# Attention in one kernel: four PSUM banks for scores, three single banks for transposed scores, exponentials one head at a time

## The reference

```python
N_HEADS = 32; N_KV = 8; HEAD_DIM = 8; N_GROUPS = 4      # 4 query heads share a key-value head
q = einsum('bsd,ed->bse', x, Wq) ...; k, v likewise; q, k = _apply_rope(q, k, s)
scores = jnp.einsum('bkgqd,bkld->bkgql', qg, k) * SCALE
attn = jax.nn.softmax(scores, axis=-1)
out = jnp.einsum('bkgql,bkld->bkgqd', attn, v)
x = x + einsum('bsd,ed->bse', out, Wo)                  # x was normalised before q, k, v
```

## Time and profile before

| what | value |
|---|---|
| time, median of three runs | 1677.78 us (1677.04 to 1677.88) |
| the profiled execution | 1684.23 us, its span 1682.4 us |
| TensorE matmuls / weight loads busy | 1460.8 / 1021.4 us of the span |
| VectorE / ScalarE / GpSimd busy | 1089.4 / 846.8 / 489.9 us |
| reductions of score chunks (L918), largest group | 305.4 us, 684 ns each |
| exponentials (L1059) | 247.9 us, 1022 ns each |

### The profile page before, as it was taken

How to read it: one execution, slowest core, us unless ns; L and a number is a source line. 1 busy time by engine, 2 the same in 40 slices (tenths; PEclk the granted TensorE clock), 3 DMA queues, 4 the chain that set the end, 5 groups by cost and what they waited for, 6 DMA issues and landing times. The chain is left out here.

```text
span 1682.4 us, 24339 instructions
## 1 busy us (share of the span) xinstructions
PE 1460.8 (87%) x7712; PEld 1021.4 (61%) x7712; DVE 1089.4 (65%) x1946; ACT 846.8 (50%) x1206; POOL 489.9 (29%) x409
## 2 busy tenths in 40 slices
PE   3999369999999966999497987899999999998697
PEld 3566243333333334665386775788888887887586
DVE  4122379999999953112476775777787778777375
ACT  1222115777777741221432776666756675765332
POOL 1344310000000021443100113556556556565100
PEclk9999778999999996999799998899999999999799
DMA  8432201111111009222301002323222323231200
GB/s 298 132 49 45 56 20 23 27 27 27 27 27 27 8 22 340 45 45 40 103 1 33 26 22 82 94 76 101 80 87 85 94 77 104 68 103 38 76 1 26
DMA packets 83008, 111.79 MB, mean 66 GB/s; under 512 B 11905, under 2 KB 60801, under 8 KB 82913
## 3 DMA queue, kind: packets, MB, share of 16 engines
q1 hardware_dynamic: 73536, 96.44, 19.4%
q0 software_dynamic: 9376, 14.16, 4.8%
HBM read 89.99 MB, written 11.93 MB: 61 GB/s over the span
## 5 line engine op out<-in xcount | busy, mean ns | idle before, releaser
L918 DVE TENSOR_REDUCE attn_max_chunks<-attn_scores 128x1 f32<-128x512 f32 x488 | 305.4, 684 | 23.9 <-PE attn_scores L1147 23.8
L1059 ACT ACTIVATE attn_probs<-attn_scoresT 128x1024 f32<-128x1024 f32 x256 | 247.9, 1022 | 122.3 <-PE attn_scoresT L1163 122.1
L1147 PE MATMUL attn_scores<-attn_k_picks,attn_q_group 64*128 64x512 f32 x488 | 185.8, 462 | 10.9 <-DVE attn_max_chunks L918 2.3
L1147 PEld LDWEIGHTS attn_scores<-attn_k_picks,attn_q_group 64*128 64x128 f32 x488 | 85.0, 190 | 173.2 <-DVE attn_max_chunks L918 164.8
L1577 DVE SCALAR_TENSOR_TENSOR ssm_scan_x<-ssm_scan_proj,ssm_w_conv,ssm_scan_x 128x1023 f32<-128x1023 f32 (+2 forms) x96 | 123.0, 1282 | 79.5 <-ACT ssm_scan_x L1572 73.8
L1163 PE MATMUL attn_scoresT<-attn_q_group,attn_k_picks 64*128 64x512 f32 x512 | 151.7, 433 | 3.3 <-ACT attn_probs L1059 3.3
L401 DVE TENSOR_TENSOR moe_h<-moe_silu,moe_up 128x512 f32<-128x512 f32 x46 | 31.7, 688 | 188.4 <-PE moe_up L516 188.4
L1175 PE MATMUL attn_o<-attn_probs,attn_v_group 128*32 128x512 f32 x1024 | 138.0, 611 | 0.4 <-ACT attn_probs L1059 0.3
L62 PE MATMUL ssm_scan_proj<-ssm_xnT_hi,ssm_w_in_hi 128*128 128x512 f32 x256 | 109.6, 428 | 23.2 <-DVE ssm_scan_x L1577 21.4
L448 ACT ACTIVATE moe_silu<-moe_gate 128x512 f32<-128x512 f32 x46 | 27.5, 597 | 199.6 <-PE moe_gate L516 199.6
L286 POOL DMA_INDIRECT moe_sums<-moe_y,moe_token x46 | 72.7, 1581 | 164.8 <-DVE moe_y L410 158.9
(11 more groups left out here) (338 smaller groups left out, 3193.1 us busy)
## 6 DMA issues: line engine op xcount, KB each, us to landing
ssm_cum_all<-ssm_cums SPq DMA_DIRECT2D x32, 512.0 KB, 3.8
ssm_scan_exp_cum<-ssm_cums SPq DMA_DIRECT2D x32, 512.0 KB, 3.7
moe_w_gate_up<-in_moe_w SPq DMA_DIRECT2D x16, 512.0 KB, 11.3
moe_w_up<-in_moe_w SPq DMA_DIRECT2D x16, 512.0 KB, 11.2
moe_w_down<-in_moe_w SPq DMA_DIRECT2D x16, 512.0 KB, 11.5
ssm_w_in<-in_in_w SPq DMA_DIRECT2D x64, 128.0 KB, 2.7
ssm_scan_w_out<-in_out_w SPq DMA_DIRECT2D x8, 512.0 KB, 3.8
moe_sums<-main_residual SPq DMA_DIRECT2D x2, 1024.0 KB, 5.6
```

The lines of the kernel that those rows point to most:

```text
L918: return nc.vector.tensor_reduce(rmaxc[:, half, place:place + 1], chunk_bank(g, n), AX_X, ALU.max).then_inc(reduced, 1)
L1059: nc.scalar.activation(probs[s % 2][:, 2 * pair:2 * pair + 2, :], st_ps[pair][:], ACT.Exp, scale=SCALE).then_inc(exp_done, 1)
L1147: nc.tensor.matmul(chunk_bank(g, n), qs[b][head_rows(j), t * P:(t + 1) * P], kz[b][head_rows(j), j % 2, c * BANK:(c + 1) * BANK], start=Tr ...
```

## The change

The pair banks for transposed scores become three single banks, and the bank that this frees is the fourth for chunks. Each transposed-scores matmul now signals for itself, and each exponential reads one head (128x512), four to a slot. The heads of the transposed scores and of the values matmuls are ordered by `T_TURNS`. A slot's order on TensorE becomes: head 0, chunk, head 1, chunk, head 2, chunk, values of the slot before, head 3, chunk. The banks of the lead-in are given out anew, and in the last group ScalarE reads the first final transposes (`last_high(0)`) one slot later.

```diff
+T_TURNS = (2, 0, 3, 1)
-        st_ps = [sp.ps(f"scoresT{b}", [P, 2, BANK]) for b in range(2)]
+        st_ps = [sp.ps(f"scoresT{b}", [P, BANK]) for b in range(3)]
+        fourth_ps = sp.ps("scores3", [P, BANK])
-        ring = [mx_ps[0], mx_ps[1], third_ps]
+        ring = [mx_ps[0], mx_ps[1], third_ps, fourth_ps]
-        bank_of, free_from = {}, [0, 1, 2]
+        bank_of, free_from = {}, [0, 1, 2, 3]
-            free_from[bank] = k + 3
+            free_from[bank] = k + len(ring)
+        st_bank, st_before = [], []
+        for k in range(GQ * SLOTS):
+            st_bank.append(1 if k == GQ * SLOTS - 1 else k % 3)
+        for k in range(GQ * SLOTS):
+            back = 1
+            while st_bank[k - back] != st_bank[k]:
+                back += 1
+            st_before.append(back)
-            return n % 2 if n >= LEAD_SCORES_T else (3, 5, 0, 1, 4, 6)[n % 6]
+            return (0, 1, 3)[n % 3] if n >= LEAD_SCORES_T else (4, 5, 0, 1, 6, 3)[n % 6]
...
-                    sync.wait_ge(scoresT_done, 2 * SLOTS * (g - 1))
+                    sync.wait_ge(scoresT_done, GQ * SLOTS * (g - 1))
...
-            def exp_pair(g, s, pair):
+            def exp_head(g, s, i):
                 n = SLOTS * g + s
-                act.wait_ge(scoresT_done, 2 * n + pair + 1)
-                if not (isinstance(n, int) and n < 2):
+                act.wait_ge(scoresT_done, GQ * n + i + 1)
+                if i == 0 and not (isinstance(n, int) and n < 2):
                     act.wait_ge(pv_done, n - 1)
-                nc.scalar.activation(probs[s % 2][:, 2 * pair:2 * pair + 2, :], st_ps[pair][:], ACT.Exp,
+                nc.scalar.activation(probs[s % 2][:, i, :], st_ps[st_bank[GQ * s + i]][:], ACT.Exp,
                                      scale=SCALE).then_inc(exp_done, 1)
...
-                    if last and s == KT_TILES + 1:
+                    if last and s == KT_TILES + 2:
                         last_high(0)
...
-            def scoresT(g, b, s, pair, after=None):
+            def scoresT(g, b, s, i):
...
-                    pe.wait_ge(exp_done, 2 * n - 1 + pair)
+                    pe.wait_ge(exp_done, GQ * n + i + 1 - st_before[k])
+                j = T_TURNS[i]
+                nc.tensor.matmul(st_ps[st_bank[k]][:], kz[b][head_rows(j), j % 2, kt * P:(kt + 1) * P],
+                                 qs[b][head_rows(j), half_cols(half)], start=True, stop=True).then_inc(scoresT_done, 1)
...
-                pe.wait_ge(exp_done, 2 * (SLOTS * g + s) + 2)
+                pe.wait_ge(exp_done, GQ * (SLOTS * g + s) + GQ)
...
-                    scoresT(g, b, s, 0)
-                    scoresT(g, b, s, 1, jobs(2))
-                    jobs(1)
-                    if s > 0:
-                        values(g, b, s - 1)
-                    elif not first:
-                        values(g - 1, 1 - b, SLOTS - 1)
+                    for i in range(GQ):
+                        if i == GQ - 1:
+                            if s > 0:
+                                values(g, b, s - 1)
+                            elif not first:
+                                values(g - 1, 1 - b, SLOTS - 1)
+                        scoresT(g, b, s, i)
+                        jobs(1)
                     jobs(len(todo))
```

More of the change, by code:

```diff
@@ L1149, in score_chunk @@
                                  start=True, stop=True).then_inc(scores_done, 1)
-            def scoresT(g, b, s, pair, after=None):
+            def scoresT(g, b, s, i):
                 half, kt = divmod(s, KT_TILES)
-                n = SLOTS * g + s
-                if pair == 0 and kt == 0:
+                n, k = SLOTS * g + s, GQ * s + i
+                if i == 0 and kt == 0:
                     pe.wait_ge(max_in[half], 32 * (g + 1))
-                if isinstance(n, int) and n == 0:
+                if isinstance(n, int) and n == 0 and i < 3:
                     pe.wait_ge(reduced, LEAD_SCORES_T)
                 else:
-                    pe.wait_ge(exp_done, 2 * n - 1 + pair)
-                upper = after is not None and TURNS[after % GQ] < 2
-                for i in ((1, 0) if upper else (0, 1)):
-                    j = TURNS[2 * pair + i]
-                    last = nc.tensor.matmul(st_ps[pair][:, i, :], kz[b][head_rows(j), j % 2, kt * P:(kt + 1) * P],
-                                            qs[b][head_rows(j), half_cols(half)], start=True, stop=True)
-                last.then_inc(scoresT_done, 1)
+                    pe.wait_ge(exp_done, GQ * n + i + 1 - st_before[k])
+                j = T_TURNS[i]
+                nc.tensor.matmul(st_ps[st_bank[k]][:], kz[b][head_rows(j), j % 2, kt * P:(kt + 1) * P],
+                                 qs[b][head_rows(j), half_cols(half)], start=True, stop=True).then_inc(scoresT_done, 1)
             def values(g, b, s):
                 half, kt = divmod(s, KT_TILES)
-                pe.wait_ge(exp_done, 2 * (SLOTS * g + s) + 2)
+                pe.wait_ge(exp_done, GQ * (SLOTS * g + s) + GQ)
                 if s == 0:
@@ L1222, in jobs @@
                     def jobs(count):
-                        after = None
                         for kind, ahead, n in todo[:count]:
@@ L1266, in _ @@
                 score_chunk(0, 0, n)
-            for bank in range(3, 7):
+            for bank in range(4, 7):
                 held.pop(bank)
```

20 lines of the change are left out of this document (9 added, 11 removed).

## The result

The changed kernel takes 1685.63 us (median of 7 runs, 1681.03 to 1690.64), the kernel before 1677.78 in the same comparison (7 runs, 1675.53 to 1678.96). The ratio is 1.0037, 95% interval 1.0023 to 1.0051: slower by 0.37%. The forecast was 1675.0, the other way. A second comparison gave 1.0031 (1.0015 to 1.0046), so the sign stands.

A forecast was written before the change was run, and what follows sets the result against it. The bound was taken as a 2.70 us chain through one score bank, not a full engine. Terms -9.9, -2.6, +0.7, +8.7, +1.3 and -1.0 sum to -2.8 us, giving 1675.0 us; 8-in-10 range 1665.5 to 1684.5.

The forecast's parts named there:

- Sum: Whole kernel: the attention layer's terms add to -2.8 us, carried over to the median of the runs as 1675.0 us.
- Plain periods: Attention slots without a transposed maximum: V to V falls from 2.70 to 2.60 us on 100 periods, -9.9 us.
- Slots with a transposed maximum: 14 attention slots holding a transpose of the maxima: 2.95 us becomes 2.80 in eight and 2.70 in six, -2.6 us.
- The copy of the output: ScalarE's copy of finished output ends 0.05 us after the V that needs its bank, 14 times, +0.7 us.
- A queue that the order moves: SyncE's loads of the next group start 2.0 us later, stopping TensorE in groups 1 to 6; 1.45 us each, +8.7 us.
- The last group: Its 12 periods, without chunks from slot 5 on, go from 31.98 to 33.3 us, +1.3 us.
- The lead-in: The last eight chunks before the first slot use three banks instead of two, -1.0 us.
- the third: Rival: the stop for the loads lowers TensorE's clock, after four of six stops, +6 us, 1681; chance 0.14.
- Rival 1: The next group's loads don't stop TensorE, so the +8.7 us goes: 1666.3 us; chance 0.12.
- Rival 2: Slot loop stays at 2.70 us, from slower single exponentials or a third head further from V: 1683.3 us; chance 0.15.
- the doubled signals cost nothing: In the slot loop, twice as many completion signals add no time; the skill's 26 ns each would be some 3 us.

The follow-up runs named there:

- third chunk first: The changed kernel with a slot's third chunk issued ahead of the third head's transposed scores instead of behind them; 1680.54 us, ratio 0.9996 to the kernel before.

## Why the prediction was wrong

The step that failed is the **Sum**: it adds terms of the attention layer alone and carries all the rest over from the kernel before as it stood. No rival of mine left the layer either. The runs showed that the rest moved. The changed program is 64 instructions longer in TensorE's stream, the loop over heads behind it is then fetched again on its second turn, TensorE stands for 3.45 us and its clock falls behind that. Put into the kernel before by itself, this costs 0.20% (0.07 to 0.33), 3.4 us; taken out of the changed kernel, the ratio goes from 1.0037 and 1.0031 to 1.0016, 2.5 to 3.5 us, though the intervals overlap.

From the forecast 1675.0 to the measured 1685.63 it is 10.6 us. Some 3.4 of them are the fetching and 2.9 the layer's own terms below; the other 4 or so no experiment assigns to a cause.

Had the sum stood, the layer's own -2.8 us would still not have been there. By its terms:

- **Plain periods** (-9.9 us): the loop was right, each term of it (1.00, 0.53, 0.60, 0.43), and 2.61 was measured in the groups that are written out. In groups 1 to 6 it is 2.68: the chunk behind the third head's blocked matmul goes 0.08 later, on some 65 of the plain periods. I took the distance from the third chunk to V from a kernel in which the chunk itself was the blocked instruction.
- **The border**, which had no term: 2.97 for 2.60, seven times, +2.6 us. I took each chunk's bank as the one of a slot before; at the border it isn't, with 66 jobs on four banks.
- **Slots with a transposed maximum**: 2.73 to 2.78, forecast 2.80 and 2.70. The copy of the output adds 0.07 in some of its slots, forecast 0.05.
- **A queue that the order moves** (+8.7 us): right in its place and its cause, and in both its times (1.53 and 16.2 behind V). Only its price was off: 0.7 per group, +4.2 us, since what comes in front of it is longer by the first two items. When the first was taken away (third chunk first), it was 1.0 to 1.1 per group; the two trade against each other.
- Between V(1) and V(115) all this makes 312.82 us (267.28 to 580.10) where it was 311.48 (270.18 to 581.65): +1.3, forecast -3.1.
- **The last group**: 33.33 us, forecast 33.3. Right.
- **The lead-in**: V(1) comes 71.9 us behind the layer's start where it was 74.5, -2.6 us, forecast -1.0.

-2.6 + 1.3 + 1.4 is the +0.1 us of the stretches.

Of the rivals, the third (a low clock behind a stop) was seen in one stop of six in three of seven profiles, 1.6 to 2.6 us each time: under 1 us on average and not 6. Rival 1 (no stop) was not met. Rival 2 (2.70, because the third head is further from V than the chunk is now) named the cause that was found, 0.08 of its 0.1 us, but only where thresholds are in registers: 2.68 there, 2.61 elsewhere. I had given it 0.15. That the doubled signals cost nothing was right: from the transposed scores to the exponential that waits for them it is 0.04 us, with one head to a signal as with two. The Trainium skill, "TensorE: Matmul & The Clock Gate", section "The cost: per-tile semaphore tail", would have had them cost; the trace after shows no such increment. For the exponential, the Trainium skill, "ScalarE: Activation LUTs", section "What ACT_TABLE_LOAD costs", gives an estimate of 0.61 us; 0.599 was measured.

What stays open: the changed kernel without the fetching still lies at 1.0016, which is 2.7 us with an uncertainty of the same size, so whether it is slower by something small isn't settled. The changed kernel with 60 instructions of padding came out at 1.0056, above the unpadded one. Its profile shows where: 2.0 us more at the jump, with two stops for one, some 3 us more at the end of the attention layer, and two heads of the scan longer by 2.3 and 2.5 us. Only the first has a cause here.

## What to carry to other kernels

A change to the length of one engine's program moves all code behind it, and a loop behind it that was kept may then be fetched again on each turn. Compare the instruction packets in the list of queues between two profiles, and look for a wait on "issue" at the jump back of each loop; a few instructions of padding in idle time tell whether that is it. And before judging a change by its layer's own profile, compare the lengths of the layers that it doesn't touch.

When the number of buffers in a ring changes, check that it divides the number of jobs to a turn of the loop. And in a loop with thresholds in registers, an instruction behind one that blocks came 0.08 us late here, which I take for its own threshold's arithmetic: put the one whose wait is long met in front.

## What the runs showed of the hardware that was not expected

- A loop of 1123 TensorE instructions, 70 KB, was kept over its second turn or fetched again depending only on where it lay: 50 or 51 packets of 16 KB against 59 or 60, 34.5 us against 37.6 to 39.7 for the two heads at the jump.
- The refetch shows as one stop on "issue" of 3.4 to 3.9 us on TensorE (loop at 212 or 214), or two of 2.2 to 2.7 (at 16 or 18), with a spell of the lower clock (1.2 GHz) behind it: in the changed kernel 0.95 granted over the two heads, 1.00 without.
- Behind a blocked matmul the next one came 0.08 us later where its threshold is in a register (2.68), and not where the program is written out or the order is turned (2.61). That it is the arithmetic is inferred from these two.
- An instruction that only waits, for two semaphores that are met, has a record of 0.051 us, but one follows another every 0.108 us.
